# Four column strips for the attention products, the causal products right behind them, and three queues reordered

## What is computed

```python
xn = _layernorm(x)
# first branch: Q, K, V = xn @ WQ, WK, WV in 16 heads of 16, causal mask, softmax
a = (softmax(Q @ K.T / 4 + mask) @ V) @ WO
# second branch, heads h, experts e
q, k = rope(xn @ Wq[h]), rope(xn @ Wk[h])
gv, go = gate(xn, Wsel_v), gate(xn, Wsel_o)       # sigmoid, the best 2 of 8
v = sum_e gv[h, e] * (xn @ Wv[h, e])
o = softmax(q @ k.T / 8) @ v
src2 = sum_h sum_e go[h, e] * (o @ Wo[h, e])
s = ln1(xn + src2)
out = x + a + ln2(s + relu(s @ W1 + b1) @ W2 + b2)
```

## Time and profile before

| | us |
|---|---|
| median of 3 runs | 3394.34 (3392.23 to 3401.13) |
| profiled execution | 3397.84 |
| its span, first to last instruction | 3395.7 |
| TensorE busy | 3205.2 (94%) |
| VectorE, ScalarE, GpSimd busy | 2491.7, 2011.8, 1580.6 |

### The profile page before, as it was taken

How to read it: one execution, slowest core, us unless ns; L and a number is a source line. 1 busy time by engine, 2 the same in 40 slices (tenths; PEclk the granted TensorE clock), 3 DMA queues, 4 the chain that set the end, 5 groups by cost and what they waited for, 6 DMA issues and landing times.

```text
span 3395.7 us, 65565 instructions
## 1 busy us (share of the span) xinstructions
PE 3205.2 (94%) x18624; PEld 2406.3 (71%) x18624; DVE 2491.7 (73%) x4716; ACT 2011.8 (59%) x4637; POOL 1580.6 (47%) x1295
## 2 busy tenths in 40 slices
PE   1699999999999999999999999999999999997997
PEld 1577777777777777777777777777777777775886
DVE  6577777777777777777777777777777777775776
ACT  2466666666666666666666666666666666664443
POOL 4144355445444454335533554434544543345666
PEclk9999999999999999999999999999999999998999
DMA  5233333233333332333332332333333423324122
GB/s 167 69 77 87 88 94 87 69 84 102 84 84 84 85 100 75 79 89 101 77 85 71 101 99 66 87 98 88 84 80 73 117 71 82 87 63 122 63 81 75
DMA packets 116487, 295.24 MB, mean 87 GB/s; under 512 B 33889, under 2 KB 54625, under 8 KB 100065
## 3 DMA queue, kind: packets, MB, share of 16 engines
q1 hardware_dynamic: 116448, 294.78, 32.8%
HBM read 262.74 MB, written 31.98 MB: 87 GB/s over the span
## 4 chain that ended last, share of the span: by engine, by line
PE 82%; DVE 7%; issue 6%; ACT 3%; DMA 1%; POOL 1%; ACTq 0%; SPq 0%; DVEq 0%; POOLq 0%
PE bank L710 29%; PE bank L836 22%; PE bank L755 9%; PE bank L810 7%; PE bank L725 5%; PE bank L730 3%; PE bank L782 2%; PE bank L952 2%; PE bank L791 2%; DVE uf L1310 2%; ACT probs L1016 2%; DVE oo L1303 1%; PE bank L731 1%; PE bank L963 1%; ACT pt_e L1036 1%
## 5 line engine op out<-in xcount | busy, mean ns | idle before, releaser
L579 POOL TENSOR_TENSOR u_l<-uf,u_h 128x512 fp32r<-128x512 f32 x512 | 716.4, 1410 | 718.2 <-ACT u_h L1100 718.1
L1207 DVE TENSOR_REDUCE nmax<-bank 128x1 f32<-128x512 f32 (+3 forms) x1024 | 552.4, 580 | 305.6 <-PE bank L725 300.6
L710 PE MATMUL bank<-wv_h,xx 128*128 128x512 f32 x2048 | 754.9, 410 | 7.1 <-DVE vm L1228 7.1
L1016 ACT ACTIVATE probs<-bank,nmax 128x512 f32<-128x512 f32 (+3 forms) x1024 | 590.6, 609 | 254.1 <-DVE nmax L1207 254.1
L1100 ACT ACTIVATE u_h<-uf 128x512 fp32r<-128x512 f32 x512 | 321.8, 632 | 702.4 <-DVE uf L1310 686.9
L710 PEld LDWEIGHTS bank<-wv_h,xx 128*128 128x128 f32 x2048 | 386.3, 189 | 155.3 <-issue 59.6
L575 POOL TENSOR_TENSOR v_sb<-v_next,zero_hb 128x512 f32<-128x512 f32 x64 | 74.3, 1160 | 891.2 <-PE bank L810 875.9
L755 PEld LDWEIGHTS bank<-ident_sb,probs 128*128 128x128 f32 x3328 | 389.0, 141 | 106.7 <-issue 51.5
L755 PE MATMUL bank<-ident_sb,probs 128*128 128x128 f32 x3328 | 452.5, 274 | 1.6 <-ACT stackT L1091 0.9
L836 PE MATMUL bank<-u_h,wo_h 128*128 128x512 f32 x1024 | 427.9, 418 | 7.8 <-ACT u_h L1100 6.3
L1310 DVE TENSOR_TENSOR uf<-oo,go 128x512 f32<-128x512 f32 x512 | 421.4, 833 | 9.1 <-POOL u_l L579 6.9
(11 more groups left out here) (167 smaller groups left out, 5622.8 us busy)
## 6 DMA issues: line engine op xcount, KB each, us to landing
go<-go_d SPq DMA_DIRECT2D x256, 512.0 KB, 6.5
xx<-xs_d SPq DMA_DIRECT2D x128, 512.0 KB, 3.6
oo<-scale_d SPq DMA_DIRECT2D x128, 128.0 KB, 2.9
a_d<-a_out SPq DMA_DIRECT2D x128, 128.0 KB, 2.3
pt_c<-in_x SPq DMA_DIRECT2D x16, 512.0 KB, 4.7
st<-in_wv SPq DMA_DIRECT2D x16, 512.0 KB, 5.7
st<-in_wo SPq DMA_DIRECT2D x16, 512.0 KB, 7.3
go_d<-go_turned SPq DMA_DIRECT2D x256, 8.0 KB
```

The costliest lines, as they stand in the source:

```text
L579: nc.gpsimd.tensor_tensor(u_l[:, e % 2], uf[:, e % 2], u_h.bitcast(f32)[:, e % 2], ALU.subtract).then_inc(ul_done, 1)
L710: last = nc.tensor.matmul(out, lhs, rhs, start=n == 1, stop=n == 3 * len(chunks))
L1016: nc.scalar.activation(probs[:, s % 2, j, 0:w], sbank[j][:, 0:w], ACT.Exp, bias=nmax[:, 2 * s + j:2 * s + j + 1], **kw).then_inc(exp_done, 1)
L1207: nc.vector.tensor_reduce(nmax[:, 2 * s + j:2 * s + j + 1], sbank[j][:, 0:w], AX.X, ALU.max, negate=True).then_inc(nmax_ready, 1)
```

## The change

Four things are moved or cut differently; nothing else is computed. AT is cut into strips of 32 columns: 16 matmuls of 32 columns instead of 8 of 64. AC moves from slot 1 to the end of slot 0, directly behind AT, and its copy on ScalarE stands between the first and the second UH. V 1 moves from slot 2 to slot 1 on TensorE. U 2 moves ahead of CH 1 on VectorE, and on GpSimd UL 3 ahead of the first pair of rotary products. The order of the jobs on the two banks stays the same.

```diff
-PE_FILL = [[("P", 0), ("P", 1), ("P", 2), ("P", 3), ("AT", 0)],
-           [("AC", 0), ("V", 0)],
-           [("J", 0), ("V", 1), ("J", 1)],
+PE_FILL = [[("P", 0), ("P", 1), ("P", 2), ("P", 3), ("AT", 0), ("AC", 0)],
+           [("V", 0), ("V", 1)],
+           [("J", 0), ("J", 1)],
            [("V", 2), ("J", 2), ("J", 3)],
            [("V", 3), ("J", 4), ("V", 4)],
...
-ACT_FILL = [[("P", 0), ("P", 1), ("P", 2), ("P", 3), ("EX", 0), ("UH", 0), ("UH", 1)],
-            [("AC", 0), ("VA", 0), ("PA", 0)],
+ACT_FILL = [[("P", 0), ("P", 1), ("P", 2), ("P", 3), ("EX", 0), ("UH", 0), ("AC", 0), ("UH", 1)],
+            [("VA", 0), ("PA", 0)],
             [("UH", 2), ("UH", 3), ("VN", 0)],
...
 DVE_FILL = [[("CH", 0), ("ON", 0), ("U", 0), ("U", 1)],
-            [("CH", 1)],
-            [("U", 2), ("V", 0), ("U", 3)],
+            [("U", 2), ("CH", 1)],
+            [("U", 3), ("V", 0)],
             [("V", 1), ("U", 4), ("V", 2), ("U", 5)],
...
              [("UL", 0), ("UL", 1)],
-             [("UL", 2), ("RP", 0), ("UL", 3)],
+             [("UL", 2), ("UL", 3), ("RP", 0)],
              [("RP", 1), ("UL", 4), ("RS", 0)],
...
                     for k in range(TT):
                         for j in range(2):
-                            mm = nc.tensor.matmul(o[j * P:(j + 1) * P, :], v_sb[:, k, j, :], pt_e[:, j, k, :], start=k == 0, stop=k == TT - 1)
+                            for c in range(0, P, STRIP):
+                                mm = nc.tensor.matmul(o[j * P + c:j * P + c + STRIP, :], v_sb[:, k, j, c:c + STRIP], pt_e[:, j, k, :], start=k == 0, stop=k == TT - 1)
```

## The result

The changed kernel takes 3408.55 us in the median (3407.64 to 3410.27), the kernel before 3394.34: a ratio of 1.0034, 95% interval 1.0022 to 1.0045. So it is slower by 14 us, outside of what could be noise, and on the side that was forecast (3416, with 3407 to 3425 as the forecast's own range). The profiled execution took 3407.64 us, its span 3405.7, where those of before were 3397.84 and 3395.7.

The account below looks back on a forecast made before the run. TensorE was taken to bound the kernel, with a side chain next to it deciding at mix 4. There 0.35 us more a pass, times 62 passes, gave 22 us on the median: 3416 us, own range 3407 to 3425.

Parts of the forecast that it names:

- What bounds: Whole kernel: TensorE busy 94% of the span, its only large wait 43.3 us at the scores of slot 3.
- the side chain: Beside TensorE: value copy, U, high half, low half, CH 1 and row maxima; its lateness at mix 4 decides the forecast.
- Parts 1 and 2: TensorE, AT and AC: strips cost 0; AC right behind AT saves one change of tile form, 0.11 us.
- Part 3: TensorE, slot 1: two value tiles bring scores 3 to +9.70 and the 0.73 us wait there to 0.
- Part 4: VectorE: U 2 ahead of CH 1 is held by the second low half; row maxima 3 come 0.91 us late.
- Part 5: GpSimd: UL 3 ahead of the rotary pair; one interruption (0.42) goes, UL 4 ends at +22.64, mix 3 gains 0.16.
- the sum: TensorE at mix 4: it waits for UL 4 and counts as +22.87 against +22.47; 0.35 us a pass taken.
- the signs: Profile after: line 730 waits nearly gone, mix 4 waiting 0.8 us a pass, a pass of 46.9 to 47.0 us.
- slow restart: TensorE at mix 4: starting after a wait for its low half loses 0.08 us.
- the two interruptions that were left: GpSimd's queue, third to fifth low half: U 4 and U 5 still interrupt it, 0.42 and 0.53 us.
- (b): Rival, VectorE: U 2 gets the port between the first and second low half; -0.08 us a pass, 3389 us; 17%.
- (a): Rival, TensorE: the wait at scores 3 goes and mix 4 isn't late; 0.62 us less a pass, 3355 us; 21%.

Follow-up runs that it names:

- e2: The kernel before with only AT cut into strips of 32 columns: 3396.62 us, ratio 1.000.
- e6: The kernel of e4 with AT in 64 columns again: 3338.05 us, against 3329.80 for e4 on the same chip.
- e7: The kernel of e4 with the second value tile (V 1) back in slot 2 on TensorE: 3410.78 us, ratio 1.0039.
- e5: The changed kernel with GpSimd's second low half computed for only 8 of its 512 columns: 3357.64 us, ratio 0.988.
- e1: The changed kernel with U 2 back behind row maxima 3 on VectorE: 3363.02 us, ratio 0.9905.
- e4: The kernel of e1 with the first pair of rotary products moved to the beginning of GpSimd's pass: 3329.25 us, 3329.80 when run again.

## Why the prediction was right

**What bounds.** Right for the pair loop. The wait that was read at line 730 went, and the side chain that stood next to TensorE took over at mix 4. Of the whole program line 730 wasn't the only large wait: the turns of the input (line 696) waited 69.4 us, eight times, all in the first 85 us, and 70.1 us after the change, so they play no part.

**Parts 1 and 2, strips and AC.** Right: 3.57 us alone (e2), AC with no change of form behind AT, turn 0 at +4.65 and scores 2 at +5.67, both as forecast. The Trainium skill ("TensorEngine Tiling (Array Packing)", section "Theoretical Speedup") gives up to 4x where a dimension is 32 or less. The prediction read it as a promise for AT, but AT's 64 columns cut into two strips are still 64, and each strip streams the same columns again; e2 (3.57 us against 3.58) and e6 show no halving. The value of a change of form was taken from two matmul distances as 0.11 and is 0.13 to 0.15 (e6). The forecast +4.65 lies 0.14 below AT and AC added up (3.58+1.21) and not 0.11, so it fits e6 better than the term beside it. In the changed kernel, where mix 4 waits for the low half, it should bring nothing; no run shows that.

**Part 3, two value tiles.** Right: scores 3 forecast at +9.70, measured at +9.63, no wait; e7 shows that the cover is the tile's.

**Part 4, U 2 ahead of CH 1.** The step that decides, and right to 0.02 us up to row maxima 3: U 2 issued at +7.87 (forecast 7.88), ended at +9.37 (9.37), CH 1 at +9.30 (9.29), row maxima 3 at +13.00 (12.98), scores 4 waiting 0.43 (0.42). The last of these is luck in part: scores 4 were to start with the third high half at about +14.30. That half came at +14.15, and scores 4 still at +14.31, right behind the exponentials, which the profile names. e5 takes the running low half away and with it 0.83 of the 0.91.

The Trainium skill's rule ("SBUF — State Buffer", section "SBUF: two separate sides") says that the loser of the port blocks fully: e5 agrees, U 2 takes 1.50 beside a low half and 0.68 without one. The other direction agrees too. U 5 ran from 1645.28 to 1645.96 in the changed kernel; the low half that began with it ended 1.14 after that, where it takes 1.28 alone. So the loser ends after the winner by about its own length less 0.13, whichever engine it is on.

**Part 5 and the sum.** The mechanism was right and the size was off: 0.18 us a pass instead of 0.35, just under the forecast's own 0.2 to 0.5. So that the time fell in 3407 to 3425 is luck in part: 11 us of longer passes on the median of before give 3405, and the medians happen to lie 14 apart. Two of the signs were missed as well: a pass of 46.78 and not 46.9 to 47.0, and a wait of 0.53 at mix 4 and not 0.8. Two terms were mis-sized. The third high half was held at a fixed distance from row maxima 3, to come at +14.33. In the kernel before, it was U 2 that it came behind (U 2 ended at +13.38, the high half came at +13.42), and U 2 stood behind row maxima 3. With U 2 moved ahead that bond is gone, and it came at +14.15, right behind the exponentials: 0.18 less, which reaches the fifth low half; that ended at +22.41 instead of +22.64 in this pass, at +22.45 in the mean. e1 and e5 bear it out: the distance is 1.35 with U 2 behind row maxima 3 and 1.15 with U 2 ahead. And mix 4 starts 0.10 after its low half, not 0.15. Mix 4 was forecast at +22.79 before the cost of its slow restart and came at +22.55 in the mean, 0.24 earlier. 0.40 less 0.24 is 0.16, and the pass shows 0.18. The restart itself (0.31 to the second matmul) is there as counted, and so are the two interruptions that were left: at the third rotary product (1.20) and in the fifth low half (1.82).

**The rivals.** U 2 between the two low halves (b) didn't happen: U 2 was issued at +7.87, 0.33 after the second one had begun. The full gain (a) was near: e1 has it for two lines of one table, -33 us where the rival had -39. It needed U 2 out of the way of the port, not a port that can be shared.

## What to carry to other kernels

An engine's wait that is taken away brings only the distance to the chain that comes next, so follow that chain with the change in place before moving anything else: here one job (U 2), moved up by one slot, met a running job of another engine, and jobs of three engines behind it came late. When VectorE and GpSimd both read SBUF, look at what runs on the other one at the very moment; such a job belongs where the other is idle (e4 gained 34 us over e1 by putting 1.5 us of GpSimd work into a gap of 13). And where a job waits for two things at once, write down both: if the change moves one, the fixed distance to the other isn't fixed.

## What was not expected of the hardware

When VectorE's product and GpSimd's next operation come up at the same time, either can win. In the changed kernel U 4 is issued at +17.99 to +18.10, within 0.02 us of the start of the second rotary product. In 49 of 62 passes it loses and takes 1.28 us, as in the pass shown above, and GpSimd is held up only at the next product (1.20 at line 589). In the other 13 it takes 0.68, and the second product is held up. Such a pass (AT at 923.06), VectorE and GpSimd:

```profile
941.14 0.68 DVE L1311 TENSOR_TENSOR uf<-oo,go 128x512 f32<-128x512 f32 x1
```

```profile
940.44 0.74 POOL L586 TENSOR_TENSOR rot<-raw,rope_sb 128x256 f32<-128x256 f32 x1
941.14 1.29 POOL L587 TENSOR_TENSOR rot<-raw,rope_sb 128x256 f32<-128x256 f32 x1
```

The second rotary product takes 1.29 instead of 0.75. The fifth low half ends 4.35 us after U 4's issue in the first case and 4.45 after it in the second, so passes of one loop differ by 0.1 us with nothing else changed.

Two more figures are the same wherever they were measured (the kernels before and after, e1, e4 and e5). A low half that is held by a U ends 1.14 to 1.16 after it (1.28 alone), and a U that is held by a low half ends 0.55 to 0.56 after that (0.68 alone). How much an operation grows then depends on how long the other one had run when it started: the rotary product that began 0.09 after U 4 in the kernel before grew by 0.42, the low half that began 0.02 after U 5 by 0.53. Why the last 0.13 of the length overlaps, no run here shows.
